# Attention plus FP4 feed-forward on one Trainium2 core: four tiles' attention from spread values, residuals preset in PSUM behind gate products, products in place of two idle stretches, and a drain turned on TensorE

## The reference, cut to what matters

```
x = x + xattn(layernorm(x), ctx, ctx, Wq, bq, Wout, bout)
#   q, k, v = (.. @ Wq + bq) (16 wide); corr = mean over batch and head of ifft(fft(q) conj(fft(k)))
#   top 12 lags of the 128, softmax -> weights; R = sum of w * roll(v, -lag)
#   broadcast R over 16 heads, reshape, @ Wout + bout
x = x + ffn(layernorm(x), w_gate, w_up, w_down)
#   fp4(a): a block of 16 is divided by max|a| / 6, rounded to the grid 0 .5 1 1.5 2 3 4 6, scaled back
#   gate, y = fp4(x) @ fp4(w_gate).T, fp4(x) @ fp4(w_up).T          (704 wide each)
#   h = silu(gate) * y;   out = fp4(h) @ fp4(w_down).T              (256 wide)
```

## Time and profile before

| | |
|---|---|
| three runs | 478.62, 478.89, 481.21 us |
| profiled execution | 479.78 us, span 477.3 us |
| TensorE (PE) busy | 445.2 us, 93% of the span, mean granted clock 0.982 |
| VectorE (DVE) busy | 436.4 us, 91% |
| ScalarE (ACT) busy | 384.4 us, 81% |
| GpSimd (POOL) busy | 248.5 us, 52% |
| chain that ended last | PE 80%, DVE 9%, ACT 3%, DMA 3%, issue 2% |

### The profile page before, as it was taken

One profiled execution on the slowest core, in us unless ns is written; L12 is line 12 of the kernel. 1 busy time (PEld: TensorE's weight loads), 2 busy tenths in 40 slices (PEclk: granted clock), 3 DMA queues, 4 the chain that ended last, 5 costly groups with the idle time before them and its releaser, 6 DMA issues.

```text
span 477.3 us, 9868 instructions
## 1 busy us (share of the span) xinstructions
PE 445.2 (93%) x3362; PEld 300.8 (63%) x3362; DVE 436.4 (91%) x768; ACT 384.4 (81%) x642; POOL 248.5 (52%) x338
## 2 busy tenths in 40 slices
PE   4599995978699999999999999999999999999987
PEld 4488885844366666666666666666666666666675
DVE  3699987579999999999999999999999999999982
ACT  3369969599988888888888888888888888867572
POOL 4157750544466655665555666666666655433310
PEclk9799997999999999999999999999999999999999
DMA  7999901442256678656567666676666666555565
GB/s 242 339 349 347 345 13 33 90 90 67 59 116 138 139 121 159 128 126 129 129 130 139 140 134 139 132 134 131 139 139 137 140 116 141 107 105 106 119 139 129
DMA packets 164849, 68.66 MB, mean 144 GB/s; under 512 B 129216, under 2 KB 164544, under 8 KB 164800
## 3 DMA queue, kind: packets, MB, share of 16 engines
q1 hardware_dynamic: 164800, 68.03, 62.2%
HBM read 27.38 MB, written 9.18 MB: 77 GB/s over the span
## 4 chain that ended last, share of the span: by engine, by line
PE 80%; DVE 9%; ACT 3%; DMA 3%; issue 2%; SPq 1%; POOL 1%; DVEq 0%; POOLq 0%; ACTq 0%
PE ps L889 16%; PE ps L890 15%; PE ps L891 15%; PE ps L899 15%; PE ps L901 8%; PE ps L903 3%; PE ps L740 2%; PE ps L750 2%; DMA ctx_sb<-in_ctx_dram 2%; PE ps L763 2%; DVE a_bst L994 1%; ACT h_c L565 1%; DMA hqT<-ctx_sb 1%; ACT h_c L562 1%; DVE hb L1145 1%
## 5 line engine op out<-in xcount | busy, mean ns | idle before, releaser
L889 PE MATMUL ps<-guT_hi,a_xT 128*128 128x512 f16 (+1 forms) x384 | 139.5, 363 | 7.9 <-DVE hb L1145 5.4
L890 PE MATMUL ps<-guT_lo,a_xT 128*128 128x512 f16 (+1 forms) x384 | 139.5, 363 | 0.0
L891 PE MATMUL ps<-guT_hi,a_xT 128*128 128x512 f16 (+1 forms) x384 | 139.4, 363 | 0.0
L899 PE MATMUL ps<-dT_hi,hqT 128*128 128x256 f16 x704 | 129.2, 273 | 2.6 <-DMA hqT<-ctx_sb 2.6
L901 PE MATMUL ps<-dT_lo,hqT 128*128 128x256 f16 x384 | 87.3, 273 | 0.0
L492 POOL TENSOR_TENSOR ctx_sb<-w_q_lo,sl 128x704 f16<-128x704 f16 x58 | 87.2, 1524 | 0.0
L621 ACT ACTIVATE w_raw<-ps,inv_gu 128x704 f32<-128x704 f32 x64 | 53.9, 841 | 33.4 <-PE ps L891 33.3
L899 PEld LDWEIGHTS ps<-dT_hi,hqT 128*128 128x128 f16 x704 | 68.9, 98 | 13.7 <-DMA hqT<-ctx_sb 3.7
L508 POOL TENSOR_TENSOR sl<-bm,sh 128x240 f16<-128x240 f32 (+2 forms) x34 | 20.5, 604 | 95.0 <-DVE y_h L1241 72.8
L889 PEld LDWEIGHTS ps<-guT_hi,a_xT 128*128 128x128 f16 x384 | 37.7, 98 | 45.8 <-DMA a_xT<-ctx_sb 8.6
L562 ACT ACTIVATE h_c<-y_h 128x1408 bf16<-128x1408 bf16 (+3 forms) x39 | 47.9, 1227 | 20.1 <-DVE y_h L1241 16.6
(11 more groups left out here) (164 smaller groups left out, 794.9 us busy)
## 6 DMA issues: line engine op xcount, KB each, us to landing
xs<-in_x_dram SPq DMA_DIRECT2D x16, 512.0 KB, 8.4
ctx_sb<-in_ctx_dram SPq DMA_DIRECT2D x16, 512.0 KB, 7.9
out_dram<-a_xT SPq DMA_DIRECT2D x64, 128.0 KB, 2.2
w_raw<-a_scratch SPq DMA_DIRECT2D x60, 128.5 KB, 2.7
hqT<-ctx_sb SPq DMA_TRANSPOSE x64, 3.8
w_raw<-in_L_ffn_w_down_dram SPq DMA_DIRECT2D x1, 704.0 KB, 8.3
w_raw<-in_L_ffn_w_gate_dram SPq DMA_DIRECT2D x1, 640.0 KB, 5.0
w_raw<-in_L_ffn_w_up_dram SPq DMA_DIRECT2D x1, 640.0 KB, 6.3
```

Source lines behind the costliest of these rows:

```text
L889: pe.matmul(dst, xt[:, c, :], guT[0][:, c, n0:n1], start=(c == 0), stop=False)
L890: pe.matmul(dst, xt[:, c, :], guT[1][:, c, n0:n1], start=False, stop=False)
L891: last = pe.matmul(dst, xt[:, KC + c, :], guT[0][:, c, n0:n1], start=False, stop=(c == KC - 1))
L899: last = pe.matmul(dst, hqT[:, j % 4, c, :], dT_hi[:, c, :], start=(c == 0), stop=(added(j) and c == DCH - 1))
```

## The change

It changes all five engines' programs.

- **Opening.** The reciprocals of the down weights move behind the last `evac_qk`; the first scaling step of the top-k is folded into the exponential; ScalarE evacuates the values ahead of its weight splits, loads its Silu table before the evacuations, and evacuates the weight fills in three parts between the `w_hi`. The fills get other banks (`GU_BANK`), so that a fill waits for an evacuation four back. The 8 filler products in front of line 867 go; 10 stand behind the first four fills and 10 behind the fifth.
- **Attention of tiles 0 to 3.** GpSimd adds the bias to the four tiles and writes their values spread over 128 rows (`v_head`); TensorE multiplies these by `wp` itself (`attend_head`, two products a tile), ahead of and between the four `attend`; `pick` and its four products and the wait for a_sb go.
- **Residual.** Of the tiles 2 to 55, those with i % 4 != 1 are preset: a product opens the bank inside `gate_and_up` between its second and third bank (`open_down`; its result is overwritten), ScalarE writes the scaled x into the bank (`preset_x`), and `down` accumulates on it. Every fourth tile (1, 5, ..., 53) stays with VectorE. Tiles 56 to 61 have the fp32 product in front of the wait for the turned h; tile 0 keeps it at the end.
- **Drain.** In stage 31 `split_h` runs ahead of the second `silu`; the products of pair 30 are written tile by tile on VectorE; the last pair's h is turned by TensorE in five parts, four evacuated by ScalarE (`keep_turned`), one by VectorE, and VectorE evacuates both last tiles.
- Waits are renumbered, `residual` of an odd tile moves ahead of `silu(2st)` on ScalarE, three of the down weights' five evacuations come later, the fillers ahead of the first gate product become 20 from 28.

```diff
 DA = D + 1
 FIRST, END = -4, NP + 4
-A_BANK = (4, 6, 0, 1)
-PICK_BANK = (2, 3, 5, 7)
...
+HEAD_BANK = (3, 4, 5, 7)
+GU_BANK = (0, 1, 2, 3, 6, 0, 1, 2)
 N_PIECES = 4
+CUT = FF // P
+PARTS = ((0, CUT), (CUT, DCH), (CUT, CUT + 3), (CUT + 3, DCH))
+TURNS = ((0, 0), (0, 1), (1, 0), (1, 2), (1, 3))
+TURN_BANK = (0, 1, 3, 4, 5)
...
         def added(i):
-            return i % 2 == 1 and i // 2 < NP - 4
+            return i % 4 == 1 and i // 2 < NP - 4
...
+        def preset(i):
+            return i >= 2 and i % 4 != 1 and i // 2 < NP - 4
...
+        def turned(k):
+            t, part = TURNS[k]
+            c0, c1 = PARTS[part]
+            return bank16(TURN_BANK[k])[:, 0:c1 - c0, :], hqT[:, (2 * NP - 2 + t) % 4, c0:c1, :]
...
-                               channel_multiplier=1).then_inc(s["pick_set"], 1)
+            pool.wait_ge(s["late_loaded"], 32)
+            pool.wait_ge(s["trx"], 2)
+            pool.tensor_tensor(xs[:, 0:4, :], xs[:, 0:4, :], bout_bc[:, 0:D].unsqueeze(1).broadcast_to([P, 4, D]), ALU.add)
+            pool.wait_ge(s["trc"], 2 * NQ)
+            pool.wait_ge(s["v_ev"], 2)
+            for two in range(2):
+                last = pool.tensor_copy(
+                    v_head[:, two].rearrange("p t (h r) -> p t h r", r=ROWS8),
+                    v_all[:, 0:4 * DH].rearrange("p (t r two) -> p t r two", t=4, two=2)[:, :, :, two].unsqueeze(2).broadcast_to(
+                        [P, 4, HEADS, ROWS8]))
+            last.then_inc(s["spread_v"], 1)
+            pool.wait_ge(s["m_sums"], 2)
+            pool.tensor_tensor(neg_mean[:, 0:4], neg_mean[:, 0:4], bout_bc[:, D:DA].broadcast_to([P, 4]), ALU.add
+                               ).then_inc(s["head_sum"], 1)
             w_lo(N_GU)
...
+            for g in range(2):
+                keep_v(g)
             w_split(N_GU)
             w_split(N_GU + 1)
-            for g in range(2):
-                keep_v(g)
             act.wait_ge(s["t_steps"], 3)
-            act.activation(wexp[:, :], corr[:, 0, 0:P], ACT.Exp, bias=nmx[:, 0:1]).then_inc(s["t_exp"], 1)
-            evacuate_weights(act, range(GU_FILLS))
+            act.activation(wexp[:, :], bank(4)[:, 0:P], ACT.Exp, bias=nmx[:, 0:1], scale=1.0 / (B * DH)).then_inc(s["t_exp"], 1)
+            act.preload_act_table(ACT.Silu)
+            evacuate_weights(act, range(EARLY))
             w_hi(N_GU)
+            evacuate_weights(act, range(EARLY, EARLY + 1))
             w_hi(N_GU + 1)
-            act.preload_act_table(ACT.Silu)
+            evacuate_weights(act, range(EARLY + 1, GU_FILLS))
...
+            def keep_turned(k):
+                act.wait_ge(s["z_turn"], k + 1)
+                act.wait_ge(s["d_done"], 2 * NP - 5 + TURNS[k][0])
+                src, dst = turned(k)
+                act.activation(dst, src, ACT.Copy).then_inc(s["z_ev"], 1)
...
+            def preset_x(i):
+                if preset(i):
+                    act.wait_ge(s["o_open"], n_preset(i))
+                    act.activation(bank(6 + i % 2)[:, 0:D], xs[:, i, :], ACT.Copy, scale=out_fac[:, 0:1]).then_inc(s["o_set"], 1)
...
+                    residuals(2 * st - 7)
                     silu(2 * st)
+                    preset_x(2 * st - 6)
...
+                    if st == NP - 1:
+                        split_h(j)
+                    silu(2 * st + 1)
+                    preset_x(2 * st - 5)
+                    if st < NP - 1:
+                        split_h(j)
+                    split_x(n)
...
                     last_split(0)
-                    residual(2 * st - 6)
-                    residual(2 * st - 5)
+                    residual(2 * NP - 7)
+                    residual(2 * NP - 6)
+                    residual(2 * NP - 5)
                     last_split(1)
-                elif st > NP + 1:
-                    residuals(2 * st - 8)
-                    residuals(2 * st - 7)
+                    keep_turned(0)
+                    keep_turned(1)
+                    residual(2 * NP - 4)
+                    keep_turned(2)
+                    keep_turned(4)
+                    residual(2 * NP - 3)
...
+            def filler(n):
+                pe.wait_ge(s["v_ev"], 2)
+                for _ in range(n):
+                    pe.matmul(bank(5)[:, 0:P], ones[:, :], ident[:, :], start=True, stop=True)
...
+            filler(10)
             pe.wait_ge(s["w_pool"], 2)
             pe.wait_ge(s["g_io"], 32)
             pe.wait_ge(s["qk_ev"], NO)
             pe.matmul(bank(4)[:, 0:P], ones[:, :], dg[:, :], start=True, stop=True).then_inc(s["t_pe"], 1)
             pe.wait_ge(s["w_lo"], N_GU)
-            for f in range(EARLY, GU_FILLS):
+            transpose_weights(EARLY)
+            filler(10)
+            for f in range(EARLY + 1, GU_FILLS):
                 transpose_weights(f)
...
+            def attend_head(j):
...
+                        pe.wait_ge(s["t_steps"], 9 + h)
+                    last = pe.matmul(bank(HEAD_BANK[j])[:, 0:DA], v_head[:, h, j, :], wp[:, h, :], start=(h == 0), stop=(h == 1))
+                last.then_inc(s["direct"], 1)
+            def attend(g):
+                pe.wait_ge(s["w_ev"], EARLY + g + 1)
+                for h in range(2):
                     last = pe.matmul(bank(A_BANK[g])[:, 0:DA], v_rows[:, P * g:P * (g + 1), h], wp[:, h, :],
                                      start=(h == 0), stop=(h == 1))
...
+            pe.wait_ge(s["spread_v"], 1)
+            pe.wait_ge(s["w_ev"], EARLY)
+            attend_head(0)
+            attend_head(1)
+            attend(0)
+            attend_head(2)
+            attend_head(3)
+            for g in range(1, 4):
+                attend(g)
...
-                dst = bank(6 + j % 2)[:, 0:D]
-                pe.wait_ge(hT[j % 4], 16 * (j // 4 + 1))
-                out_ready(pe, j - 2)
+                final = j // 2 == NP - 1
+                late = j >= 2 * (NP - 4) and not final
+                dst = bank(2 * (1 - j % 2) if final else 6 + j % 2)[:, 0:D]
+                if final:
+                    if j % 2 == 0:
+                        turn_last(0)
+                elif preset(j):
+                    pe.wait_ge(s["o_set"], n_preset(j))
+                else:
+                    out_ready(pe, j - 2)
+                if late:
+                    pe.matmul(dst, ident_out[:, :], xs[:, j, :], start=True, stop=False)
+                if not final:
+                    pe.wait_ge(hT[j % 4], 16 * (j // 4 + 1))
                 for c in range(DCH):
-                    last = pe.matmul(dst, hqT[:, j % 4, c, :], dT_hi[:, c, :], start=(c == 0), stop=(added(j) and c == DCH - 1))
+                    if final and j % 2 == 0 and c in (0, CUT):
+                        if c:
+                            turn_last(1)
+                        pe.wait_ge(s["z_ev"], 2 if c else 1)
+                    if final and j % 2 == 1 and c in (0, CUT, CUT + 3):
+                        if c == CUT:
+                            pe.wait_ge(s["z_ev_v"], 1)
+                        else:
+                            pe.wait_ge(s["z_ev"], 4 if c else 3)
+                    last = pe.matmul(dst, hqT[:, j % 4, c, :], dT_hi[:, c, :], start=(c == 0 and not late and not preset(j)),
+                                     stop=(c == DCH - 1 and j > 0))
...
-                if not added(j):
+                if j == 0:
                     last = pe.matmul(dst, ident_out[:, :], xs[:, j, :], start=False, stop=True)
...
+            def turn_last(t):
+                for k in range(len(TURNS)):
+                    if TURNS[k][0] == t:
+                        dst = turned(k)[0]
+                        c0, c1 = PARTS[TURNS[k][1]]
+                        pe.wait_ge(s["z_done"], 2 * t + (1 if c0 == 0 else 2))
+                        for c in range(c0, c1):
+                            last = pe.transpose(dst[:, c - c0, :], hq[:, (NP - 1) % 2, t, c * P:(c + 1) * P], ident16[:, :])
+                        last.then_inc(s["z_turn"], 1)
...
-            for _ in range(28):
+            for _ in range(20):
                 pe.matmul(bank(4)[:, 0:P], ones[:, :], ident[:, :], start=True, stop=True)
...
                 gu_bank(i, 0)
                 gu_bank(i, 1).then_inc(s["gate_done"], 1)
+                if i >= 8:
+                    open_down(i - 6)
                 gu_bank(i, 2).then_inc(s["gu_done"], 1)
+            def open_down(j):
+                if tile_ok(j) and preset(j):
+                    out_ready(pe, j - 2)
+                    pe.matmul(bank(6 + j % 2)[:, 0:D], ident16[:, :], dT_hi[:, 0, :], start=True, stop=False).then_inc(s["o_open"], 1)
...
-                    w_prepare(1)
+                    w_sizes(1)
             evac_qk(NO - 1)
+            w_inverses(1)
...
-            dve.tensor_scalar(corr[:, 0, 0:P], bank(4)[:, 0:P], 1.0 / (B * DH), None, ALU.mult).then_inc(ts, 1)
-            dve.memset(corr[:, 1, P:P + 4], big)
+            dve.max(top[:, 0, :], bank(4)[:, 0:P]).then_inc(ts, 1)
             dve.wait_ge(ts, 1)
```

(69 more changed lines are left out.)

119 lines of the change are left out of this document (57 added, 62 removed).

## The result

The changed kernel takes **476.8 us** (median of 11 runs, 474.9 to 478.0), the kernel before beside it 479.7 (478.5 to 481.4): ratio 0.9932, 95% interval 0.9912 to 0.9951. So it is faster by 0.7 to 1.1%, 3 to 5 us. Forecast were 470.7 us and a range of 467.8 to 475.2: the direction was right, the size was not, and the result lies outside the range. The profiled execution has a span of 474.4 us, 2.9 less than before.

The account below looks back on a forecast made before the run. The prediction took TensorE (11.277 us a stage) and VectorE (11.304) to bound the kernel together. Steady part -5.2, opening -1.3 and drain -1.75 summed to -8.2 us, from the median 478.89 to 470.7 us, range 467.8 to 475.2.

Parts of the forecast that it names:

- What bounds the kernel now: Steady stretch: TensorE at 11.277 us a stage and VectorE at 11.304 are both full; a shorter stage must relieve both.
- Residual, TensorE, 11.01 us: Steady stage: one line 903 goes (0.43 us), opening products add 0.16, so TensorE's stage falls from 11.277 to 11.01 us.
- Residual, VectorE: Steady stage: 28 residuals of 0.39 us become 14, so VectorE's mean stage falls from 11.304 to 11.11 us.
- Residual, ScalarE, 0.40 a preset: Steady stage: each preset costs ScalarE 0.40 us; its work rises from 9.8 to 10.6 us and fits under 11.11.
- Rival (c): ScalarE's presets in the steady stage cost more than idle time covers; at 1.0 us each, 480.6 us; chance 0.05.
- The added wait: TensorE's opening product inside gate_and_up waits for ScalarE's evacuation; VectorE still sets the rhythm at 11.11 us; steady part -5.2.
- rival (b): Steady stage: the ring binds, stages stay at 11.28 us, only opening and drain pay: 475.9 us; chance 0.12.
- The ring of 10.8 to 11.2 us: Steady-stage loop of evacuation, opening product, gate products, silu and splits: 10.8 us, 11.2 with the odd preset before split_h.
- Opening, -1.3: Before the steady stretch: cT's product and heads' products come earlier, VectorE is free at 90.2 us; saves 1.3 us.
- Rival (a): TensorE's clock falls to 1.2 GHz in the opening, costing 2.4 us: 473.1 us; chance 0.16.
- Drain, -1.75: At the end: TensorE turns the last pair's h instead of waiting for DMA; last evacuation at 472.9 us; saves 1.75.
- Sum: Whole kernel: steady part -5.2, opening -1.3 and drain -1.75 make -8.2 us, giving 470.7 us.

Follow-up runs that it names:

- e2: Changed kernel without GpSimd's addition of the attention's output to x (output lacks the attention from tile 4 on): 469.9 us, ratio 0.9791 to the kernel before.
- e4: Changed kernel with the residual of every odd tile on VectorE again, every even tile preset: 476.4 us, ratio 0.9935 to the kernel before.
- e6: Changed kernel with 28 fillers and, in stages without a residual on VectorE, one tile's half of GpSimd's addition on VectorE: 472.7 us, ratio 0.9856.
- e8: The changed kernel itself, run again in a later session: 475.8 us beside 481.0 for the kernel before, ratio 0.9894.

## Why the prediction was wrong, step by step

- **What bounds the kernel now.** Two engines full at 11.277 and 11.304, and both must be relieved: right. But GpSimd, which sets when VectorE's product may run, was left out. The earlier trace rows has it at 169 of 280 us, and that looked like slack. Its 1.18 us stood at the one place of the stage where cover is short.
- **Residual, TensorE, 11.01 us.** Right: 11.02 in e2, where TensorE binds.
- **Residual, VectorE, "Half a residual a stage goes: 11.304 - 0.195 = 11.11 us": this is the step that failed.** It took an instruction's duration for the price of its removal. The path there was `x_c`, GpSimd's addition, product (2.0 us), not residual, reciprocal, product. The price of the step was 5.2 us of the 8.2. Where the addition is gone the step is right: 11.18 us with the residual and 10.79 without in the changed kernel's stages behind the 25, and 11.18 and 10.86 in e2, where TensorE's 11.02 sets the mean. By e4 it is worth 0 where the addition stays. The kernel before could have told it: its first stages have no residual on VectorE yet and take 11.30 us too (scaling of h at 113.45, 124.75 and 136.05). In one of them, VectorE and GpSimd:

```profile
134.11 0.90 DVE L1266 RECIPROCAL bm<-bm 128x120 f32<-128x120 f32 x1
134.92 0.87 DVE L1150 TENSOR_TENSOR ctx_sb<-x_c,sh 128x512 f16<-128x512 f16 x1
```
```profile
134.33 1.18 POOL L548 TENSOR_TENSOR xs<-xs,w_raw 128x512 f32<-128x512 f32 x1 [1.55 <-DVE x_c L949]
```

- **Residual, ScalarE, 0.40 a preset.** Right: 0.467 us busy, 0.40 from start to start (line 722 at 258.42, the next at 258.82), no stage longer by it. Its work is 10.6 us a stage as forecast (262.51 of 280 us); the prediction's own subtraction (11.30 less 0.54 and 0.86) gives 9.9 for the stage before, not 9.8. Rival (c), the slower side, is out.
- **The added wait, rival (b).** The ring of 10.8 to 11.2 us doesn't bind in e2 (11.02). TensorE does wait for ScalarE's evacuation at the opening product, 9 times 0.17 to 0.18 us from 140 to 420 us, as the prediction named it, but behind VectorE's stage. The terms of 0.15 and 0.2 us between engines have no row of their own. The changed kernel has the steady stretch of rival (b), 11.3 a stage, and nearly its time (475.9), by another cause.
- **Opening, -1.3.** Everything up to the first gate product came as worked out or better: 80.66 (forecast 80.9), 82.03 (82.2), the last addition at 89.26 (89.45), `largest_x` 89.79 (90.2), the first gate product at 98.56 for 100.32 before. The failing words are "Fewer fillers ... in front of the first gate product, which waits for DMA: nothing": in the first profile 1.6 of the 1.8 us were given back by the clock, and the maximum of h (line 1385) began at 108.65 where it began at 108.86. Rival (a), the fall between 77 and 88 us, did not come in this execution (1.00 throughout) but in those of e4 and e6, and cost 1.3 us. Its own 2.4 does not follow from its words: half of 16 products at 0.44 more, and 0.5, are 4.0. So the opening is worth the forecast's -1.3 where no clock falls (e8: first scaling of h at 112.18 for 113.45 before, -1.27), -0.6 with the fall of (a) (e4, 112.81) and -0.2 with the one at the gate products.
- **Drain, -1.75.** Right: 21.50 to 19.71 us, -1.8. The turns wait for ScalarE once, 0.46 us.
- **Sum.** In the first profile the drain begins 1.1 us earlier (453.14 to 452.05): opening 0.2, the three stages without an addition 0.8, the 25 stages before them 0.1 (282.57 to 282.50). The drain adds 1.8: 2.9 us, the difference of the spans, where 8.2 were forecast.

## What to carry to other kernels

Before an instruction is taken off a full VectorE, see what ran beside it on GpSimd: if an instruction of GpSimd with operands in SBUF is longer than the cover that remains, the saving turns into a longer duration of the next instruction with two SBUF operands. Such a hold-up shows in no list of waits here; it shows as one shape with two durations (0.36, 0.47, 0.87 us for the same 512 elements), so compare durations of equal instructions between stages before costing an edit. Where the two must meet, put GpSimd's instruction beside VectorE's reciprocals, reductions and reads of PSUM, and size it to fit there, even if VectorE does part of its work.

## What the runs showed of the hardware that was not expected

The same VectorE product (128x512, fp16) takes 0.36 us alone, and up to 0.87 beside GpSimd's addition; GpSimd's 128x512 addition takes 1.18 us alone and 2.44 if it starts under VectorE's 1408-element scaling. In the kernel before, the first sign of it was there to be read: the product took 0.47 in the steady stretch, 0.87 in stages 1 to 3, which have no residual yet, and 0.37 at the end, where GpSimd has nothing to add. TensorE at 0.50 after 3.0 us of idle time in front of the first gate product was seen in three of five executions with 20 fillers: the same idle time does not always lower the clock. In two of the eight profiled executions of the changed kernel and its variants the clock fell to 0.50 at the product with cT and the heads' products instead (from 80.5 to 84 us) and cost 1.3 us; the fall at the gate products cost 1.5.
